# A prefetch hint for the loop-closing branch on all five engines of a cross-attention kernel

## The reference

```
q = x @ Wq + bq;  k = ctx @ Wk + bk;  v = ctx @ Wv + bv
attn = softmax(q k^T / sqrt(32) + mask)          # per head, 4 query heads share one k, v
y = (attn v) @ Wo + bo + x
out = layernorm(y) * gamma + beta
```

## Time and profile before

| what | value |
|---|---|
| runs | 1966.59, 1968.9, 1969.82 us; median 1968.9 |
| profiled execution | 1968.75 us, its span 1966.2 us |
| PE busy | 1693.7 us (86%) |
| DVE busy | 1506.7 us (77%) |
| ACT busy | 1224.2 us (62%) |
| POOL busy | 544.6 us (28%) |
| granted TensorE clock, mean | 0.928 |
| data DMAs | 74.0% of 16 engines' span, 217 GB/s |

### The profile page before, as it was taken

How to read it: one execution, slowest core, us unless ns; L and a number is a source line. 1 busy time by engine, 2 the same in 40 slices (tenths; PEclk the granted TensorE clock), 3 DMA queues, 4 the chain that set the end, 5 groups by cost and what they waited for, 6 DMA issues and landing times. The chain is left out here.

```text
span 1966.2 us, 44571 instructions
## 1 busy us (share of the span) xinstructions
PE 1693.7 (86%) x14080; PEld 1143.8 (58%) x14080; DVE 1506.7 (77%) x2776; ACT 1224.2 (62%) x2877; POOL 544.6 (28%) x408
## 2 busy tenths in 40 slices
PE   4478598999889998899889998899889999998675
PEld 3245265676566765566556665566556666665254
DVE  3267688789868887788968897788968898878823
ACT  2256567666757667666757667666767668766621
POOL 2124232212622126112522126121432126200500
PEclk9689599999889998999999998999899999999678
DMA  9789888877697677876797777877687687954232
GB/s 197 200 225 268 247 228 242 268 205 205 190 294 226 183 198 274 233 215 186 226 288 225 187 216 256 246 211 196 209 271 251 197 225 230 282 178 152 93 133 107
DMA packets 314861, 425.94 MB, mean 217 GB/s; under 512 B 160736, under 2 KB 181216, under 8 KB 314592
## 3 DMA queue, kind: packets, MB, share of 16 engines
q1 hardware_dynamic: 314592, 422.69, 74.0%
HBM read 321.92 MB, written 100.66 MB: 215 GB/s over the span
## 5 line engine op out<-in xcount | busy, mean ns | idle before, releaser
L1121 PE MATMUL bank<-ring_hi,w_sb 128*128 128x512 f32 x2560 | 883.5, 410 | 88.7 <-issue 39.2
L961 ACT ACTIVATE probs<-bank,shift 128x512 f32<-128x512 f32 x1024 | 692.6, 688 | 214.8 <-DVE shift L1034 179.6
L1034 DVE CUSTOM_DVE_ANT_0 bank<-bank,mask_l 128x512 f32<-128x512 f32 x1024 | 685.4, 707 | 165.9 <-PE bank L1160 160.1
L1043 DVE STREAM_TRANSPOSE turned_p<-probs 128x2048 f32<-128x2048 f32 x256 | 586.0, 2301 | 156.0 <-PE bank L1211 125.8
L1121 PEld LDWEIGHTS bank<-ring_hi,w_sb 128*128 128x128 f32 x2560 | 494.5, 195 | 260.7 <-issue 112.9
L1121 PE MATMUL bank<-ring_lo,w_sb 128*128 128x512 f32 x1280 | 517.8, 405 | 0.0
L1160 PE MATMUL bank<-k_stack,q_stack 96*128 96x512 f32 x1024 | 409.0, 446 | 81.5 <-ACT probs L961 55.4
L1211 PE MATMUL bank<-turned_p,v_all 32*32 32x512 f32 x8192 | 315.7, 635 | 63.7 <-DVE turned_p L1043 37.4
L847 POOL TENSOR_TENSOR ring_lo<-x_t,ring_hi 128x512 fp32r<-128x512 f32 x176 | 224.0, 1285 | 396.6 <-ACT ring_hi L906 396.6
L1160 PEld LDWEIGHTS bank<-k_stack,q_stack 96*128 96x128 f32 x1024 | 196.8, 199 | 227.1 <-ACT probs L961 108.8
L1121 PEld LDWEIGHTS bank<-ring_lo,w_sb 128*128 128x128 f32 x1280 | 250.4, 196 | 49.0
(11 more groups left out here) (38 smaller groups left out, 748.4 us busy)
## 6 DMA issues: line engine op xcount, KB each, us to landing
w_sb<-w_d SPq DMA_DIRECT2D x296, 512.0 KB, 5.3
q_stack<-q_hi_d SPq DMA_DIRECT2D x128, 256.0 KB, 4.5
w_d<-w_sb SPq DMA_DIRECT2D x40, 512.0 KB, 4.8
x_raw<-in_ctx_dram SPq DMA_DIRECT2D x128, 128.0 KB, 3.8
x_raw<-in_x_dram SPq DMA_DIRECT2D x128, 128.0 KB, 4.0
q_hi_d<-part_hi SPq DMA_DIRECT2D x64, 256.0 KB, 4.7
q_lo_d<-part SPq DMA_DIRECT2D x64, 256.0 KB, 5.7
v_all<-v_d SPq DMA_DIRECT2D x256, 64.0 KB, 2.4
```

The costliest lines, as they stand in the source:

```text
L961: nc.scalar.activation(probs[:, st % 2, h, :], S_ps[h][:, :], ACT.Exp, scale=-1.0, bias=shift[:, g % 2, i:i + 1], accum_out=sums[:, g % 2, ...
L1034: nc.vector.tensor_tensor_reduce(out=S_ps[h][:, :], in0=S_ps[h][:, :], in1=mask_l[:, st, :], scale=-1.0, scalar=HIGHEST, op0=ALU.add, op1= ...
L1043: nc.vector.transpose(turned_p[:, :, :, st, :].rearrange("p j h c -> p h j c"), probs[:, st % 2, :, :].rearrange("p h (j c) -> p h j c", c ...
L1121: mm = nc.tensor.matmul(C[c][:, :], w, xx[:, slot(source, d), :], start=(n == 0), stop=(n == 23))
```

## The change

One line. The loop is made with the general `nc.Fori` in place of the engine's own, for the same one engine, with `hint_back_edge=True`:

```
             for g in range(NG):
                 for back, e in at("first", None, "mid", g):
                     do(-back, e)
-            with eng.Fori(1, NB - 1) as t:
+            with nc.Fori(1, NB - 1, engines=[eng.engine], hint_back_edge=True) as t:
                 for g in range(NG):
                     for n, (back, e) in enumerate(at("mid", "mid", "mid", g)):
                         do(Count(t, 1, -back, 1000 * g + n + 1 if afresh else 0), e)
```

## The result

The kernel with the hint takes 1980.77 us (median of 5 runs, 1978.93 to 1985.67), the kernel before in the same comparison 1969.82 us (5 runs, 1966.59 to 1974.10). The ratio is 1.0055, 95% interval 1.0037 to 1.0073: 11 us slower, where 18 us faster was predicted. The profiled execution took 1985.67 us, its span is 1983.8 us; it was the longest of the five, so marks in it are read against each other more than against the median.

A forecast was written before the change was run, and what follows sets the result against it. TensorE (PE), with work in flight 1693.7 of 1966.2 us, was taken to bound the kernel. 1968.75 - 20 (stalls removed) + 0.2 (hints) + 1.5 (wrong hint at exit) = 1950.45, so 1950.5 us; range 1942 to 1968.

The forecast's parts named there:

- The stall and its cure: At the loop's five taken branches, PE's records of about 4.9 us would fall to about 0.1 to 0.3 us.
- Rival A: No effect: the hint, armed early, is dropped or displaced and branches stay at 4.9 us; 1969 us, chance 0.12.
- The low estimate of the hint's own price: One hint instruction at the body's top per engine, six times: 0 to 0.5 us added, 0.2 taken.
- Removed, 20 us: Five waits for the body's first instructions on PE, DVE, ACT and SP go; 20 us, between measured 18.0 and 22.2.
- the same work once without a taken branch: Iteration 1, entered from above, as model: 53.1 us mark to mark against 55.7 to 58.2 over the branches.
- of its 5.2 us only 2.8 come back, and that is already in the 53.1: SP's stall at the second branch: ctx loads done 21.7 us after the mark at entry, 24.5 after the branch.
- Rival B: Stall goes, but queued transfers make PE wait instead; half the direct idle time, 7 us, stays won: 1962, chance 0.08.
- the entry's 4.4 us: Argument against gains being given back: the entry to iteration 1 has the same queue yet is 4.4 us quicker.
- The exit, 1.5 us: Wrong hint after batch 6, where the branch isn't taken, makes one fetch late, once; 1.5 us added.
- The bound, one taken branch's price of 4.4 us: Upper limit for the wrong hint at the loop's exit: 22.2 / 5 = 4.4 us.
- code already at hand runs on: Reason for a wrong-hint price nearer to none: code behind the exit branch runs while the next piece comes.
- Rival C: Slower: the hinted piece displaces the one after the body's first, 4.4 us six times; 1995 (or 1975), chance 0.07.

The follow-up runs named there:

- Experiment 1: Changed kernel with all five engines' hint outcome read from a register (taken in iterations 1 to 5, not in 6): 1970.47 us, ratio 1.0006 to the kernel before.
- 6: Kernel before with the first ctx loads moved later in the batch, plus the static hint on all engines: 1938.58 us, ratio 0.9847.
- 7: Kernel before with the first ctx loads moved later, plus hints on all five engines with the outcome from a register: 1929.48 us, ratio 0.9803.
- 2: Kernel before plus the static hint on PE alone, ctx loads in their old place: 1965.22 us, ratio 0.9952.
- 4: Kernel before plus the static hint on PE, ACT, DVE and POOL, none on SP: 1968.93 us, ratio 0.998.
- 3: Kernel before plus the static hint on SP alone: 1972.13 us, ratio 1.0017.
- experiment 11: Kernel before with the first ctx loads moved later in the batch and no hint, a repeat run: 1941.32 us, ratio 0.9862.
- 8: Kernel before plus a hint on PE alone, outcome from a register, ctx loads in their old place: 1959.65 us, ratio 0.9955.
- experiment 9: Register-outcome hints on all five engines, loads in place, but the eight ctx loads at the body's head fetch a quarter of their rows: 1931.85 us, ratio 0.9825.

## Why the prediction was wrong, step by step

- **The stall and its cure: right.** 4.9 us on PE fell to 0.45, ACT and SP go on within 0.5 us, six hints an engine. Rival A is out. The low estimate of the hint's own price stands: 31 to 61 ns.
- **Removed, 20 us: wrong, and this is the step that failed.** Experiment 1 has all five stalls removed, no wrong hint, and is worth 0.0 us (1970.47 against 1970.42); PE's idle time over the branches is as long as before. The prediction took the entry as "the same work once without a taken branch". The matmuls were the same, SP's position was not: SP came to the ctx loads 9.1 us after the mark at the entry (328.88 - 319.80), 19.4 us after it at the second branch, and 14.4 us with the hint. At the entry it is 5 us earlier than even the hinted branch makes it. It comes there from batch 0, written out, and not from a body that computes its numbers; that this is the reason isn't shown (its register arithmetic from mark to branch takes 1.6 us in the kernel before, and it issues two more DMAs there). The gap was in the earlier trace rows and was read the wrong way: "of its 5.2 us only 2.8 come back, and that is already in the 53.1" took the entry's 12.63 us of loads for a price paid, and did not ask what SP would do from 14.4 us on. With the same 10 us of loads it is through at 24.3 us, 0.2 us sooner than before.
- **Rival B named this** (idle before w_sb in the 30 us behind, marks still 57 apart) and got 0.08. Its mechanism happened in full; its size, half the gain kept, was too kind. The reason given against it, the entry's 4.4 us, was the false model.
- **The exit, 1.5 us: mis-sized, about 10.** 10.3 us (after less experiment 1) and 9.1 us (6 less 7). The bound, one taken branch's price of 4.4 us, was too low because two engines are struck at different times, PE 12.5 us and SP 51 us behind the branch, for 3.7 and 5.1 us, and the two losses add up (7.1 and 4.4 us from mark to mark, less 1.5 won back between); "code already at hand runs on" is true for these 12.5 us and then ends.
- **Rival C**: its sign came true, its mechanism did not. The entry stretch is 52.3 us (53.1 before), so iteration 1 pays nothing. Behind the five taken branches PE has its new wait of 1.0 to 1.6 us, about 13 us into the body, far less than C's 4.4.
- **The sum again:** 1969.8 - 0 (removed and given back) + 0.3 (hints) + 10 (exit) = 1980, measured 1980.8. The 0 and the 10 are measured on these same kernels, so this sum is a summary and no second forecast.

The gaps of the exit follow the hint engine by engine: PE's is in the four kernels with a static hint on PE (after, 2, 4, 6), SP's in the three with one on SP (after, 3, 6), and neither is in a kernel with the register or without a hint. So do the marks. From group 6 to group 7 of batch 6 the ten kernels without a static hint on PE take 25.2 us each, the four with one 29.8 to 33.9: PE's share is 4.7 to 8.7 us. From group 0 to group 1 of the last batch the eleven kernels without a static hint on SP take 25.7 to 28.4 us, the three with one 30.6 to 32.9: SP's share is 2 us at the least, 4.4 in the kernel after. Between these marks, where PE may wait for w_sb, the kernels differ by 21.1 to 27.8 us, and that swallows or adds several us in a single profile.

In the better order the hints are worth 1.9 us a branch and not the 3.1 us of PE's idle time in experiment 11, because a wait of 1.2 us is left; these are idle times of single profiles, and the wait's cause isn't shown.

What stays open: why the medians of experiments 2, 3, 4 and 8 don't add up engine by engine, and why a hint on PE alone is 5 us better than one on all five while the loads are in their old place; and how much of experiment 9's gain comes from SP's quick issues and how much from DMA engines that have less to move.

## What to carry to other kernels

An engine that stalls may be giving a full queue time to drain: before counting a stall as a gain, follow the engine that issues DMAs to its next issue that something waits for, and see whether the queue lets it go sooner. Take the place where "the same work" runs without the stall as a model only if every engine, the DMA issuer above all, arrives there at the same distance. A static likely-taken hint on a loop of a few long iterations is wrong once, and that once cost as much (10 us) as the five right ones brought in the better order (9 us); tell it the outcome from a register, and move bulk loads away from the branch first (1969 to 1939 to 1929 us).

## What was unexpected in the hardware

- A DMA issue on SP that takes 0.32 us took up to 3.8 us in a stretch where the DMA engines' share was 1.11 (up to 4.9 us behind another branch); with a quarter of the bytes all eight behind the second branch took 0.32 to 0.35 us.
- The hint, executed about 220 us ahead of its branch, still works: 452 ns at the median on PE instead of 4938, where the branch not taken takes 88.
- A wrong hint shows nothing at the branch itself (88 ns on PE) and comes out later, in code without branch or wait: 4.6 us on PE's weight loads 12.5 us behind, 5.1 us on SP 51 us behind.
- A hint on all five engines leaves PE a wait of 1.0 to 1.9 us, 13 to 14 us behind each taken branch, which no kernel without any hint has.
